# Odd tile's gelu one period later on ScalarE, second GLU chunk before the down product on TensorE, output additions by pairs, last tile by halves

## The reference, cut to what matters

```
x = x + L2_ffn(ratio2 * sigmoid(x))     # quantised SwiGLU: silu(y Wg) * (y Wu), then Wd; 256 -> 704 -> 256
x = x + L3_ffn(ratio3 * sigmoid(x))     # microscaled int8: LayerNorm, linear 256 -> 1024, gelu, linear 1024 -> 256

# L3_ffn, r = bf16(its input)
h = mx_layernorm(r)                      # rounded to bf16
h = mx_linear(h, W1, b1)                 # both operands quantised in blocks of 32
h = mx_gelu(h)                           # rounded to bf16
h = mx_linear(h, W2, b2)
out = bf16(r + h)
```

## Time and profile before

| | |
|---|---|
| median of three executions | 473.29 us |
| the profiled execution | 472.93 us |
| its span (first to last instruction) | 471.2 us |
| mean granted TensorE clock | 0.921 |
| PE, DVE, ACT busy | 389.1, 343.8, 293.3 us |
| last layers' pipeline | from about 341 us to the end |
| `sigmoid_l3` of pairs 0, 1, 2, 3 starts at | 375.79, 396.45, 420.00, 443.26 us |

### The profile page before, as it was taken

One profiled execution on the slowest core, in us unless ns is written; L12 is line 12 of the kernel. 1 busy time (PEld: TensorE's weight loads), 2 busy tenths in 40 slices (PEclk: granted clock), 3 DMA queues, 4 the chain that ended last, 5 costly groups with the idle time before them and its releaser, 6 DMA issues.

```text
span 471.2 us, 7317 instructions
## 1 busy us (share of the span) xinstructions
PE 389.1 (83%) x2604; PEld 339.0 (72%) x2614; DVE 343.8 (73%) x511; ACT 293.3 (62%) x517; POOL 76.9 (16%) x96
## 2 busy tenths in 40 slices
PE   3998672997852999999999999999977977878674
PEld 3998640776731789999999999999845865667432
DVE  5999989695667999999999149600330796777795
ACT  6996764689870677667676675674511448383753
POOL 3000102000110431112032011280175000000000
PEclk9999797898985699999999999999987899898897
DMA  7500000000178228210614956500033000000000
GB/s 288 183 1 1 2 0 0 1 0 1 42 238 311 83 74 312 75 44 27 222 35 135 303 211 173 196 13 24 22 91 89 0 1 1 13 1 24 4 20 33
DMA packets 23669, 38.82 MB, mean 82 GB/s; under 512 B 2233, under 2 KB 18250, under 8 KB 23506
## 3 DMA queue, kind: packets, MB, share of 16 engines
q1 hardware_dynamic: 15442, 23.39, 14.9%
q10 hardware_dynamic: 5920, 8.65, 5.4%
q0 software_dynamic: 2272, 6.30, 4.4%
HBM read 33.10 MB, written 5.24 MB: 81 GB/s over the span
## 4 chain that ended last, share of the span: by engine, by line
PE 59%; DVE 22%; ACT 9%; issue 6%; DMA 2%; POOL 2%; SPq 0%; DVEq 0%; ACTq 0%; POOLq 0%; another core or an unknown queue 0%
PE bank L1499 18%; PE bank L1478 18%; PE bank L1560 5%; PE bank L1338 3%; PE bank L1550 2%; PE bank L1309 2%; DVE scr L794 2%; DVE scr L796 2%; DVE big L1158 1%; PE bank L1470 1%; PE bank L1604 1%; PE bank L1356 1%; PE bank L1583 1%; DMA v<-in_kT 1%; ACT big L702 1%
## 5 line engine op out<-in xcount | busy, mean ns | idle before, releaser
L1478 PE MATMUL bank<-big,yT 128*128 x384 | 86.7, 379 | 0.0
L594 ACT ACTIVATE yT<-bank,big 128x128 f32<-128x128 f32 x192 | 54.7, 370 | 46.9 <-PE bank L1499 44.0
L1478 PEld LDWEIGHTS bank<-big,yT 128*128 128x128 f32 x384 | 71.2, 190 | 8.7
L373 POOL DMA_INDIRECT xg<-token_rows,rowi x24 | 31.3, 1302 | 139.3 <-PE bank L1470 116.1
L357 POOL TENSOR_TENSOR small<-small 128x2 f32<-128x2 f32 (+1 forms) x9 | 9.9, 1102 | 185.5 <-DVE small L1178 81.5
L1309 PE MATMUL bank<-identf,scr 128*128 128x128 f32 x240 | 32.6, 298 | 3.8 <-DVE scr L807 3.8
L1309 PEld LDWEIGHTS bank<-identf,scr 128*128 128x128 f32 x240 | 31.8, 215 | 4.1 <-DVE scr L807 4.0
L1550 PE MATMUL bank<-y2r,qgu 128*128 128x256 f32 x192 | 30.1, 319 | 4.9 <-DVE big L1158 2.3
L1550 PEld LDWEIGHTS bank<-y2r,qgu 128*128 128x128 f32 x192 | 28.0, 223 | 6.2 <-DVE big L1158 2.5
L1499 PEld LDWEIGHTS bank<-ygT,w3T 128*128 128x128 f32 x256 | 30.8, 198 | 1.0 <-issue 0.6
L1499 PEld LDWEIGHTS bank<-ygT,big 128*128 128x128 f32 x256 | 29.8, 192 | 2.0 <-issue 1.6
(11 more groups left out here) (342 smaller groups left out, 838.7 us busy)
## 6 DMA issues: line engine op xcount, KB each, us to landing
big<-in_moe_w SPq DMA_DIRECT2D x16, 1024.0 KB
slot_outputs<-yo ACTq DMA_DIRECT2D x24, 128.0 KB
v<-in_kT SPq DMA_DIRECT2D x2, 512.0 KB, 4.5
big<-in_gateT SPq DMA_DIRECT2D x1, 1024.0 KB, 7.0
big<-in_upT SPq DMA_DIRECT2D x1, 1024.0 KB, 9.1
big<-in_downT SPq DMA_DIRECT2D x1, 1024.0 KB, 11.6
x<-in_x_bsc SPq DMA_DIRECT2D x1, 1024.0 KB, 13.6
token_rows<-y POOLq DMA_DIRECT2D x4, 256.0 KB, 7.6
```

Of the source, the lines that this page charges most:

```text
L373: gp.indirect_dma_start(out=xg[:, j % 3], out_offset=None, in_=Y1, in_offset=bass.IndirectOffsetOnAxis(ap=rowi[:, j:j + 1], axis=0)).then_ ...
L594: ins = sc.activation(hT[j % 2][:, c], ps[1 + 2 * (j % 2) + c // 4][:, (c % 4) * P:(c % 4 + 1) * P], ACT.Gelu, bias=b1s[:, c, j:j + 1])
L1478: ins = te.matmul(ps[5 + 2 * (j % 2)][:, 0:C], hT[j % 2][:, c], big[:, bass.ds(at + (W2_AT + c * C), C)], start=(c == 0), stop=(c == IC - 1))
```

## The change

It changes the order of some instructions in the pipeline of the last two layers:

- ACT: the copies of `up_l3`'s banks (`copy_u3`) are parted from the gelu. The odd tile's gelu of pass p is issued in pass p+1, just ahead of `copy_hqT`. The loads of the three tables become explicit: Silu after the sigmoids, gelu after the last silu, Sigmoid after the even tile's gelu.
- PE: `gate_up_l2(p, 1, 1)` comes ahead of `down_l3(2p - 4)`. The four `bias` products all come ahead of the first transposes of x, with 12 (before: 5) zero matmuls behind them, and 9 (before: 4) ahead of the first gate product. Passes 4 and 5 get 3 more each ahead of `down_l3` of the even tile, the last pass 8 ahead of the last tile.
- DVE: outputs of tiles 2p-5 and 2p-4 are finished together (`finish_pair`) in passes 3 and 4, where each was finished alone before.
- last tile: quantised, turned and copied in two halves (PE banks 6 and 3); its down product waits for each half apart.

```diff
@@ ACT
+            def copy_u3(i):
+                for h in range(2):
+                    act.wait_ge(s["u3_ready"], 2 * i + h + 1)
+                    if i >= 2:
+                        act.wait_ge(s["g3_ready"], i - 1)
+                    sc.activation(a3[i % 2][:, h * 512:(h + 1) * 512], ps[4 + h][:], ACT.Copy).then_inc(s["a3_ready"], 1)
+
             def gelu_l3(i):
-                for h in range(2):
...
-                    ins.then_inc(s["a3_ready"], 1)
                 act.wait_ge(s["a3_ready"], 2 * i + 2)
...
+            def copy_last(h):
+                act.wait_ge(s["q3_tr"], T + h)
+                act.wait_ge(s["d3_ready"], T - 2)
+                sc.activation(q3T[(T - 1) % 2][:, 4 * h:4 * h + 4], last_bank[h][:].bitcast(BF16)[:, 0:4 * P].rearrange("p (c t) -> p c t", c=4),
+                              ACT.Copy).then_inc(s["q3T_ready"], 1)
...
+                if 1 <= p < G:
+                    sc.preload_act_table(ACT.Silu)
                 if p >= 3:
                     copy_ob(2 * p - 5)
...
                 if 1 <= p <= G:
+                    sc.preload_act_table(ACT.Gelu_apprx_tanh)
+                if 2 <= p <= G:
+                    gelu_l3(2 * p - 3)
+                if 1 <= p <= G:
                     copy_hqT(p - 1)
-                    sc.preload_act_table(ACT.Gelu_apprx_tanh)
+                    copy_u3(2 * p - 2)
                     gelu_l3(2 * p - 2)
-                if p >= 2:
+                if 1 <= p < G:
+                    sc.preload_act_table(ACT.Sigmoid)
+                if p == G + 1:
+                    copy_last(0)
+                    copy_last(1)
+                elif p >= 2:
                     copy_q3T(2 * p - 3)
                 if 1 <= p <= G:
+                    copy_u3(2 * p - 1)
+                if p == G:
                     gelu_l3(2 * p - 1)
@@ DVE
+            def last_quant(h):
...
+                dve.wait_ge(s["q3_tr"], i - 1)
+                ve.tensor_tensor(q3[i % 2].rearrange("p (r i) -> p r i", r=HC3)[:, half], t3.bitcast(I16),
+                                 unit.unsqueeze(1).to_broadcast([P, 4, P]), ALU.mult).then_inc(s["q3_ready"], 1)
+
+            def finish_pair(i):
+                dve.wait_ge(s["ob_ready"], i + 2)
+                at = slice(i, i + 2)
+                link(ve.tensor_tensor(ob_pair, ob_pair, res[:, at].rearrange("p t c -> p (t c)"), ALU.add))
+                ve.tensor_tensor(x[:, at].rearrange("p t c -> p (t c)"), x[:, at].rearrange("p t c -> p (t c)"), ob_pair,
+                                 ALU.add).then_inc(s["x_done"], 2)
...
-                if 3 <= p <= G:
-                    finish_tile(2 * p - 5)
...
-                if 2 <= p <= G:
-                    finish_tile(2 * p - 4)
+                if 3 <= p <= G:
+                    finish_pair(2 * p - 5)
+                elif p == 2:
+                    finish_tile(0)
...
-                if p >= 2:
+                if p == G + 1:
+                    last_quant(0)
+                    last_quant(1)
+                elif p >= 2:
                     gelu_quant(2 * p - 3)
@@ PE
-            bias(0)
-            bias(1)
-            keep_clock(6, 5)
+            for p in range(G):
+                bias(p)
+            keep_clock(6, 12)
             x_to_channels(0)
-            bias(2)
-            bias(3)
             pe.wait_ge(s["l2_int"], 1)
-            keep_clock(6, 4)
+            keep_clock(6, 9)
...
                 if p < G:
                     gate_up_l2(p, 1, 0)
+                    gate_up_l2(p, 1, 1)
+                if p >= G:
+                    keep_clock(0, 3)
                 if p >= 2:
                     down_l3(2 * p - 4)
                 if p < G:
-                    gate_up_l2(p, 1, 1)
                     gate_up_l2(p, 2, 0)
...
+                if p == G + 1:
+                    keep_clock(0, 8)
+                    turn_last(0)
+                    turn_last(1)
+                    down_last()
+                elif p >= 2:
                     turn_l3(2 * p - 3)
```

More of the change, by code:

```diff
@@ L232, in bass_adaln_ffn_stack @@
         bias_banks = (3, 4, 5, 7)
+        last_bank = (ps[6], ps[3])
         def bank_of(turn):
@@ L685, in copy_hqT @@
                               ACT.Copy).then_inc(s["hq3T"], 1)
-            def gelu_l3(i):
-                for h in range(2):
-                    n = 2 * i + h
-                    act.wait_ge(s["u3_ready"], n + 1)
-                    ins = sc.activation(a3[i % 2][:, h * 512:(h + 1) * 512], ps[4 + h][:], ACT.Copy)
-                    ins.then_inc(s["a3_ready"], 1)
+            def copy_u3(i):
[4 more added lines that the diff above has]
+                    sc.activation(a3[i % 2][:, h * 512:(h + 1) * 512], ps[4 + h][:], ACT.Copy).then_inc(s["a3_ready"], 1)
+            def gelu_l3(i):
                 act.wait_ge(s["a3_ready"], 2 * i + 2)
@@ L708, in copy_ob @@
                     act.wait_ge(s["x_done"], i - 1)
-                sc.activation(ob[i % 2], ps[7][:, 0:C], ACT.Copy).then_inc(s["ob_ready"], 1)
+                sc.activation(ob[(i + 1) % 2], ps[7][:, 0:C], ACT.Copy).then_inc(s["ob_ready"], 1)
             act.wait_ge(s["ld_sgu"], 16)
@@ L1605, in down_l3, with turn_last, down_last @@
                 te.matmul(ps[7][:, 0:C], pick[:], br[:, H3:H3 + C], start=False, stop=True).then_inc(s["d3_ready"], 1)
-            bias(0)
-            bias(1)
-            keep_clock(6, 5)
+            def turn_last(h):
+                pe.wait_ge(s["q3_ready"], T + h)
+                pe.wait_ge(s["q3T_ready"], T - 1)
+                if h:
+                    pe.wait_ge(s["x_l2"], G)
+                for c in range(4):
+                    ins = te.transpose(last_bank[h][:].bitcast(BF16)[:, c * P:(c + 1) * P],
+                                       q3[(T - 1) % 2][:, (4 * h + c) * P:(4 * h + c + 1) * P], identb[:])
+                ins.then_inc(s["q3_tr"], 1)
+            def down_last():
+                pe.wait_ge(s["ob_ready"], T - 1)
+                for c in range(HC3):
+                    if c % 4 == 0:
+                        pe.wait_ge(s["q3T_ready"], T + c // 4)
+                    te.matmul(ps[7][:, 0:C], q3T[(T - 1) % 2][:, c], w3T[:, 1, c * C:(c + 1) * C], start=(c == 0), stop=False)
+                te.matmul(ps[7][:, 0:C], pick[:], br[:, H3:H3 + C], start=False, stop=True).then_inc(s["d3_ready"], 1)
+            for p in range(G):
+                bias(p)
+            keep_clock(6, 12)
             x_to_channels(0)
-            bias(2)
-            bias(3)
             pe.wait_ge(s["l2_int"], 1)
-            keep_clock(6, 4)
+            keep_clock(6, 9)
             for p in range(G + 2):
```

12 lines of the change are left out of this document (10 added, 2 removed).

## The result

| | before | changed |
|---|---|---|
| median | 474.02 us (4 executions) | 469.66 us (467.08 to 470.03, 4 executions) |
| ratio | | 0.9892, 95% interval 0.9845 to 0.9939 |
| profiled execution | 472.93 us, span 471.2 | 470.03 us, span 468.3 |
| mean granted clock | 0.921 | 0.927 |

The kernel became 4.4 us faster, where 14.4 were forecast; 469.66 lies above the range of 452.5 to 465.5. So that the stages can be compared, I count from one fixed point, DVE's copy of `w3T` (at 337.21 us before, 339.25 after: the unchanged work ahead of it took 2.0 us longer in this execution; over all profiles the copy lies between 336.96 and 339.25 us, so I count this as scatter).

The account below looks back on a forecast made before the run. The prediction took the passes to be bound by a loop through ACT and PE, not by work. Gains of 4.3 (start), 9.3 (passes), 0.4 (pairs) and 0.4 (last tile) sum to 14.4, from 473.29 to 458.9 us; range 452.5 to 465.5.

Parts of the forecast that it names:

- 9.3 us for the three: Passes 1 to 3: gains of 1.3, 4.3 and 3.7 us from the new orders on ACT and PE.
- The waits named: DVE in passes 2 and 3: 2.37 and 1.92 us for PE's gate products, 1.57 us for ACT's sigmoid.
- a loop of ACT's work: Passes: bound by a loop through ACT and PE, not by work; moving 2.34 us on ACT starts `sigmoid_l3` 2.4 us earlier.
- pass 1 ... gain 1.3, pass 2 ... gain 4.3: Passes 1 and 2: gains of 1.3 and 4.3 us from shorter DVE waits, pass 2 falling to 19.3 us.
- rival 3: Passes: PE becomes the bound at 20.8 us a pass, 2.6 us less gain in two passes, 461.5 us; chance 0.11.
- I take that the wait keeps its length and moves with the products: Start: the ownerless wait before the first gate products are taken up shifts with PE's earlier products, gaining 4.3 us.
- The term of 4.3 us: Start: gain from earlier gate products at full clock, taken between 3.7 and 4.9 us; outer bounds 0 and 9.8.
- rival 2: Start: the ownerless wait is tied to the gathers' landing, so the start gives nothing, 463.2 us; chance 0.20.
- earlier products of PE beside gathers were passed on at once: Start: argument against the wait being tied to the gathers' landing; no size given.
- No loss: Start: bias products and 12 zero matmuls (3.0 us) fill PE's idle time to 350.0 us at the latest, costing nothing.
- the granted clock stays at 1.00 from 341 to beyond 360 us: Start: sign expected in the profile after, full PE clock throughout that stretch.
- 0.8 us forecast for pass 4 and the tail: Pass 4 and end: 0.4 us from additions by pairs and 0.4 us from the last tile by halves.

Follow-up runs that it names:

- e9: The changed kernel run once more, unedited; median 463.59 us, ratio 0.9789.
- e10: The kernel before run once more, unedited; median 472.85 us, ratio 0.9993.
- e6: The kernel before with ACT's new order alone; median 461.36 us, ratio 0.9824.
- e7: The kernel before with PE's order of chunk 1 alone (its products ahead of the even tile's down product); median 465.89 us, ratio 0.9923.
- e12: e8 with chunk 1's products behind the even tile's down product again; median 456.97 us, ratio 0.9643.
- e5: The kernel before with POOL's gathers of tiles 4 to 7 held until three gate products are signalled; median 470.70 us, ratio 1.0008.
- e16: The kernel of e5 once more, on the chip of e1; median 470.24 us, ratio 0.9920.
- e3: The changed kernel with 6 zero matmuls on PE ahead of layer 2's first down product in passes 1 to 3; median 463.58 us, ratio 0.9766.
- e2: The changed kernel with PE's start as in the kernel before; median 465.68 us, ratio 0.9817.
- e1: The changed kernel with POOL's gathers of tiles 4 to 7 held until three gate products are signalled; median 462.03 us, ratio 0.9739.
- e13: The changed kernel with only the gathers of tiles 6 and 7 held until three gate products are signalled; median 462.23 us, ratio 0.9746.
- the second group: The runs e5 to e8, made on one chip that served only this group; the kernel before had a median of 470.59 us there.
- e8: e1 plus e3's zero matmuls, with the gathers of tiles 6 and 7 moved behind POOL's first power; median 456.65 us, ratio 0.9713.
- e11: e8 with output additions one tile at a time and the last tile whole; median 457.36 us, ratio 0.9644.

## Why the prediction was wrong, point by point

**The passes were right in size, and their mechanism in part.** The forecast was 9.3 us for the three; e9 against e10 gives 67.46 - 57.51 = 9.95, if the clock stays up. The waits named did go. The share of the parts was not right. The prediction gave ACT's order the sigmoid's wait and PE's order the waits for gate products (2.37 and 1.92 us). e6 shows that ACT's order takes away both. Nor was it all a loop of ACT's work: ACT's order moved 2.34 us, and pass 2 lost 4.23 (23.55 - 19.32). In the kernel before PE ran the block of down and gate products at half clock behind its 1.85 us of idle time, which cost 1.5 us (5.54 against 4.02); with the 2.34 that makes 3.9 of the 4.23. The prediction read the 2.37 us as PE's queue and did not look at the clock in it. PE's order is worth 2.3 and 0.8 us in passes 2 and 3 alone (e7), but beside ACT's only 0.7 us in all (e12). So that the sum of the passes came out has some luck in it.

The Trainium skill, ScalarE: Activation LUTs, section "What ACT_TABLE_LOAD costs", gives 2.66 us a switch. The trace does not agree, as the prediction held: the Sigmoid load at 417.80 (1.28) ends 0.05 us before the next copy.

**The term "pass 1 ... gain 1.3, pass 2 ... gain 4.3" failed by what PE's idle time does to the clock.** The prediction looked only for waits of DVE and asked of PE whether it had too much work (rival 3). It had too little: it idled 2.0 us ahead of `down_l2`, and in the profile after the clock fell both times. That gave back 1.67 us in pass 1 and 1.68 in pass 2 (against e9). In pass 2 the gap came with the change (1.05 us before); in pass 1 the kernel before has it too (2.04 us, clock at 1.00), and e5, in the old order, fell there and took 22.40 us where e16, the same kernel, took 20.72. So the loss in pass 1 is not the change's but that of a base in which the clock happened to hold. e3 shows the cause by its cure. What decides whether the clock falls in such a gap is not settled: 10 of 18 did, and e9, with the same gaps, had none.

**The start is where the forecast fell.** The step was "I take that the wait keeps its length and moves with the products". It did not: e2 and e3 have their gate product at 27.05 and 27.24 us whether PE is early or late, and e1, e13 and e16 move it by the gathers alone. The term of 4.3 us became a loss of 0.9 (e9 against e10) to 1.9 us (the first two profiles) at the first `norm_stats`. That is rival 2 (chance 0.20, 463.2 us), and e9, in which nothing else went wrong, has a median of 463.59 (the kernel before beside it 473.63). Its counter-argument, that "earlier products of PE beside gathers were passed on at once", held only for the first of them: ACT took x's transposes 0.1 us after their end in both kernels. What holds PE's completions back stays open. Shown is this much: the last of the waits (DVE's or ACT's) ends 2.0 to 3.0 us after the last gather of a long row, in the profiles of before and after and in three of the four groups, and in the second group it isn't there. Not all are held so long: silu 0 was let through at 360.96 in the kernel before, ahead of the row's end, and 1.2 us behind it in e9.

**"No loss" from the zero matmuls was wrong as well.** The sum took 0.25 us for each and a full clock. The 12 took 5.30 us in e8, 0.44 each. Here are, of the changed kernel, PE's rows from the zero matmuls ahead of the bias products (L1573) on, and the granted clock of a stretch just behind them (columns as in the earlier trace rows):

```profile
343.48 1.67 PE L1415 MATMUL bank<-zeros,identb 128*128 128x512 bf16 x7 [1.07 <-ACT g L655]
345.08 4.04 PE L1573 MATMUL bank<-cb,big 16*128 16x256 f32 x16
349.06 4.08 PE L1415 MATMUL bank<-zeros,identb 128*128 128x512 bf16 x12
```

```profile
349.00:351.00 2.00, 2.00 (x6) 0.73 (x6) 1.14 (x3) 0.00 (x0) 1.70 (x2) 0.50 0.42 123
```

PE is busy without a break, and the clock is at 0.50 all the same. x's transposes start 1.7 us after DVE's last instruction on their tiles has ended (351.30), in the kernel before 0.1 us (349.30); that is 13.7 us after the copy, 12.2 before. The sign "the granted clock stays at 1.00 from 341 to beyond 360 us" was therefore missed at 349 us.

**The rest.** A pair's two additions take 0.42 and 0.69 us, exactly as sized. In pass 3, e11 finds 0.70 us for pairs where 0.35 was counted. The last tile by halves works: from its quantisation (460.67) to `copy_ob` (464.90) it is 4.23 us instead of 5.28, a gain of 1.05. But 0.89 us is given back ahead of it, where the last tile's gelu now comes late, in spite of the pair's gain:

```profile
458.59 1.22 DVE L1242 TENSOR_REDUCE small<-big 128x32 f32<-128x1024 bf16 x1 [1.03 <-ACT big L700]
```

That step starts 17.36 us after the last `norm_stats` (458.59 - 441.23), before 16.47 (460.45 - 443.98), and PE's clock was at 0.54 between 454 and 456 us; whether that is the cause was not tried. So of the 0.8 us forecast for pass 4 and the tail, 0.17 came.

**The account.** Against the forecast's 458.5 for a profiled execution (472.93 - 14.4) the one after took 470.03, 11.5 us more: 2.0 ahead of the copy, 6.2 at the start (41.12 against 34.9), 1.7 each in passes 1 and 2, 0.6 in pass 4 and the tail, and 0.85 back in pass 3 sum to 11.4.

## What to carry to other kernels

Where a wait has no owner in the profile, find an event that it keeps its distance to, in this trace, before deciding what it moves with: here POOL's last gather stood 3.0 us ahead of DVE's release. Before waits on one engine are shared out among the parts of a change, look at the granted clock in the stretch that each of them waited for: here half a clock made up 1.5 us of what looked like a queue. When a loop gets shorter, look for the engine that will now stand idle and what its clock does afterwards, and read that gap in more than one profile: the same one cost 1.6 us or nothing. Zero matmuls that keep the clock belong where the engine waits anyway, few enough not to be in front of work that is ready.
